# Weight pieces of 1 MB stored in four column blocks: each partition's row read as four runs of 2 KB in place of one of 8 KB

## The reference, cut to what matters

```python
scores = sigmoid(x @ router_w)                     # 32 experts, 8 of them chosen per row
gate = ragged_dot(xs, w_gate, group_sizes)         # xs: rows sorted by expert; w_gate [32, 1024, 512]
up   = ragged_dot(xs, w_up, group_sizes)
down = ragged_dot(silu(gate) * up, w_down, group_sizes)   # w_down [32, 512, 1024]
routed = (down[unsort].reshape(T, K, H) * tkw[..., None]).sum(axis=1)
shared = silu(x @ sw_gate) * (x @ sw_up) @ sw_down        # one shared expert, twice as wide
```

## Time and profile before

| | |
|---|---|
| median of 3 executions | 11513.4 us (11511.07 to 11513.97) |
| the profiled execution's own time | 11510.14 us |
| its span in the profile | 11508.5 us |
| busy: PE, DVE, POOL, ACT | 97%, 40%, 38%, 25% of the span |
| mean granted TensorE clock | 0.99 |
| moved by DMA | 1487 MB, 129 GB/s over the span |

### The profile page before, as it was taken

The page is one execution under the profiler, slowest core; times in us unless marked ns, Lnnn a source line. Parts: engine busy times, 40 slices in busy tenths (PEclk is TensorE's granted clock), DMA queues, the critical chain, the costliest instruction groups (busy, mean ns, idle before and its releaser), DMA issues.

```text
span 11508.5 us, 205338 instructions
## 1 busy us (share of the span) xinstructions
PE 11219.1 (97%) x49954; PEld 9236.2 (80%) x49955; DVE 4614.2 (40%) x6242; ACT 2927.2 (25%) x3904; POOL 4352.1 (38%) x4232
## 2 busy tenths in 40 slices
PE   8999899998999999999999999999999999999998
PEld 7888677776888888888888878878887887888887
DVE  5777766664233223332323242233334324223222
ACT  1111344442222222222222232222223223222221
POOL 2666532223333333333333333333433333333332
PEclk9999999999999999999999999999999999999999
DMA  5555567664444444454544454444556545444443
GB/s 185 169 168 174 156 181 179 180 181 136 96 119 117 98 97 118 119 138 110 125 97 118 97 159 95 111 122 118 126 141 172 126 109 144 97 97 117 97 97 84
DMA packets 954681, 1487.13 MB, mean 129 GB/s; under 512 B 318494, under 2 KB 621790, under 8 KB 930756
## 3 DMA queue, kind: packets, MB, share of 16 engines
q0 software_dynamic: 212224, 620.97, 25.3%
q1 hardware_dynamic: 356964, 474.75, 13.2%
q10 hardware_dynamic: 385376, 390.15, 12.1%
HBM read 887.22 MB, written 598.24 MB: 129 GB/s over the span
## 4 chain that ended last, share of the span: by engine, by line
PE 67%; DVE 3%; DMA 2%; issue 2%; ACT 1%; DVEq 1%; ACTq 0%; POOL 0%; SPq 0%; POOLq 0%
PE pd L2083 23%; PE pg L66 7%; PE pg L67 7%; PE pu L68 7%; PE pg L68 7%; PE pu L67 7%; PE pu L66 7%; DVE w_lo L1984 2%; DMA activated<-av 2%; DVEq L1658 1%; ACT w_hi L1891 1%; DMA aq<-activated 0%; ACT x_hi L1895 0%; ACTq L1658 0%; DVE aT L2006 0%
## 5 line engine op out<-in xcount | busy, mean ns | idle before, releaser
L1853 POOL DMA_INDIRECT out_rows<-y,idx_s x528 | 860.2, 1629 | 4444.7 <-issue 4434.7
L1845 POOL DMA_INDIRECT xq<-xn_rows,idx_q x2124 | 2141.0, 1008 | 934.2 <-issue 484.5
L1895 ACT ACTIVATE x_hi<-xT 128x1024 fp32r<-128x1024 f32 x530 | 562.9, 1062 | 4549.4 <-DMA activated<-av 4390.3
L66 PE MATMUL pg<-w_hi,x_hi 128*128 128x512 f32 x4224 | 1647.5, 390 | 42.2 <-DVE x_lo L1999 31.7
L66 PE MATMUL pu<-w_hi,x_hi 128*128 128x512 f32 x4224 | 1646.1, 390 | 1.2 <-DVEq L2053 0.4
L68 PE MATMUL pg<-w_hi,x_lo 128*128 128x512 f32 x4224 | 1646.5, 390 | 0.0
L67 PE MATMUL pg<-w_lo,x_hi 128*128 128x512 f32 x4224 | 1646.4, 390 | 0.0
L68 PE MATMUL pu<-w_hi,x_lo 128*128 128x512 f32 x4224 | 1645.0, 389 | 0.0
L67 PE MATMUL pu<-w_lo,x_hi 128*128 128x512 f32 x4224 | 1644.8, 389 | 0.0
L2034 DVE SCALAR_TENSOR_TENSOR av<-pu,scale,sg 128x512 f32<-128x512 f32 x528 | 396.4, 751 | 3067.5 <-PE pu L68 2955.7
L1999 DVE TENSOR_TENSOR x_lo<-xT,x_hi 128x1024 fp32r<-128x1024 f32 x530 | 649.6, 1226 | 1535.1 <-ACT x_hi L1895 1534.9
(11 more groups left out here) (292 smaller groups left out, 14665.0 us busy)
## 6 DMA issues: line engine op xcount, KB each, us to landing
stage<-in_w_all SPq DMA_DIRECT2D x174, 1024.0 KB, 9.0
activated<-av ACTq DMA_DIRECT2D x528, 256.0 KB, 2.3
aq<-activated ACTq DMA_DIRECT2D x528, 256.0 KB, 2.6
rep<-steps ACTq DMA_DIRECT2D x192, 512.0 KB
sums<-out_rows SPq DMA_DIRECT2D x68, 512.0 KB, 7.9
out_rows<-sums SPq DMA_DIRECT2D x68, 512.0 KB, 4.0
xq<-xn_rows,idx_q POOLq DMA_INDIRECT x2124
xt<-in_x SPq DMA_DIRECT2D x64, 512.0 KB, 6.2
```

What stands on the lines that cost most here:

```text
L66: m(dst, hi, whi[:, cols], start=begin, stop=False)
L1845: g.indirect_dma_start(out=xq[q][:, n], out_offset=None, in_=xn_q, in_offset=bass.IndirectOffsetOnAxis(ap=idx_q[q][:, n:n + 1], axis=0))\
L1853: g.indirect_dma_start(out=out, out_offset=bass.IndirectOffsetOnAxis(ap=idx_s[q][:, 0:1], axis=0), in_=y[q][:], in_offset=None, compute_op ...
L1895: a.activation(x_hi[q][:].rearrange("p b (g j) -> p b g j", g=4), xT[:].rearrange("p (g b j) -> p b g j", g=4, b=KH), ACT.Copy).then_inc(x ...
```

## The change

`w_all` is stored on the host as [pieces, 4, 128, 512] in place of [pieces, 128, 2048]: the first 512 columns of all 128 partitions, then the next 512, and so on. A piece is still 1 MB in one stretch, but the row of one partition now lies in it as four runs of 2 KB, 256 KB apart. The buffers on the chip, `raw` and `stage`, keep their layout; the four kinds of load name the four runs. Nothing else is changed: the same 186 transfers, by the same queues, at the same places, with the same waits.

```diff
+def pieces(tile):
+    return tile[:].rearrange("p (a c) -> p a c", a=4)
@@ route_stage, SP
-                sp.dma_start(raw[q][:], w_all[(E + 1) * NCH + q]).then_inc(w_loaded[q], 16)
+                sp.dma_start(pieces(raw[q]), w_all[(E + 1) * NCH + q].rearrange("a p c -> p a c")).then_inc(w_loaded[q], 16)
@@ route_stage, ACT
-                a.dma_start(raw[q][:], w_all[E * NCH + q]).then_inc(w_loaded[q], 16)
+                a.dma_start(pieces(raw[q]), w_all[E * NCH + q].rearrange("a p c -> p a c")).then_inc(w_loaded[q], 16)
@@ expert_stage, SP, load
-                    sp.dma_start(stage[q][:], w_all[bass.ds(e * NCH + q, 1)]
-                                 .rearrange("a p c -> (a p) c")).then_inc(staged[q], 16)
+                    sp.dma_start(pieces(stage[q]), w_all[bass.ds(e * NCH + q, 1)]
+                                 .rearrange("z a p c -> p (z a) c")).then_inc(staged[q], 16)
@@ expert_stage, SP, before the first tile
-                sp.dma_start(stage[q][:], w_all[bass.ds(e * NCH + q, 1)].rearrange("a p c -> (a p) c"))\
+                sp.dma_start(pieces(stage[q]), w_all[bass.ds(e * NCH + q, 1)].rearrange("z a p c -> p (z a) c"))\
                     .then_inc(staged[q], 16)
@@ layouts
-        "w_all": np.concatenate([*gu, dn], axis=1).reshape(n * NCH, P, WC),
+        "w_all": np.concatenate([*gu, dn], axis=1).reshape(n * NCH, P, 4, WC // 4).transpose(0, 2, 1, 3),
```

## The result

The changed kernel took 11533.9 us (median of 19 runs, 11529.2 to 11539.7), the kernel before 11513.1 us in the runs beside it (19 runs): 20.8 us more, a ratio of 1.0019 with an interval of [1.0013, 1.0025]. The prediction was 11446 us, with a range from 11418 to 11515. It was wrong in sign, and the result lies outside the range.

What follows compares the result with a forecast made beforehand. PE, busy 97% of the span, was taken as the bound, so only its stops could be won: 23 + 9 + 14 + 15 + 4 + 5 - 3 = 67 us off 11513.4 gave 11446 us, range 11418 to 11515.

Steps and rivals of the forecast that it cites:

- Rows: In the weight loads: 186 loads of 128 rows become 186 of 512, and the four runs are not joined again.
- rival C: Weight loads: the queue joins the runs, packets stay 8 KB and nothing happens; 11513 us, chance 0.04.
- Time of a row: On a DMA engine: 84 ns per 2 KB row, so a piece takes 2.70 us in place of 2.53.
- Turns: Between DMA queues: a row waits for one row of the other queue, 84 ns with 2 KB rows.
- roomy switches: Expert switches with room around them: about 20 PE gaps of 0.5 to 1.2 us; 15 us gained.
- Standing behind: Read of `aq` behind rows already taken on: depth counted in rows, so 0.7 us in place of 2.5.
- tight switch: Where one-tile experts follow each other: 4.5 of a 5.36 us gap gained; 23 us in all, 9 for slow clock.
- Rival A: At expert switches: depth is one of bytes or time, so gaps hardly move; about 11502 us, chance 0.21.
- The tile behind: Tile after a switch between one-tile experts: gaps of 2.81 and 1.30 us and slow matmuls; 14 of 25 us gained.
- The start: Kernel start: SP's rows wait less behind ACT's loads, so DVE begins 5 us earlier, passed on whole.
- Longer loads: Weight loads: six pieces take 1.0 us more DMA time, hidden since ACT doesn't wait; 3 us charged over the span.
- Rival B: At every switch: 2 KB rows cost 129 ns, the store finds more ahead; +40 us, 11553, chance 0.13.

Runs made afterwards that it cites:

- padded rows: Changed kernel with two unused 2 KB rows behind each block, runs 260 KB apart in place of 256: 11512.3 us, 1.0003 of the kernel before.
- the burst is split: Three pieces asked for ahead, the fourth a tile later: 11478.2 us with the 8 KB rows of before, 11508.3 with the changed layout, 11491.0 with runs 260 KB apart.
- near layout: Changed kernel with a partition's four 2 KB runs side by side, 2.25 KB apart: 11516.5 us, 1.0006 of the kernel before.
- repetition: Changed kernel run once more, unaltered, in the last batch: 11535.5 us, 1.0024 of the kernel before.

## Why the prediction was wrong, step by step

- **Rows.** Right: +95232 packets; rival C is out.
- **Time of a row.** Right where nothing else runs: 392 GB/s at 3293 to 3295 us against 388 foreseen, and a median row of 84 ns.
```profile
3293.00:3295.00 2.00, 2.00 (x11) 1.65 (x10) 1.02 (x2) 0.63 (x1) 1.06 (x3) 1.00 1.02 392
```
- **Turns.** Right, and better than it was used. It was applied to ACT's transfers against SP's loads. For POOL the text said that its gathers and adds "get a larger share beside loads: nothing but safety". **This is the first step that failed.** A larger share for POOL is a smaller one for the pieces, and the store stands behind the pieces. With padded rows, where the turns are left and the distance is not, the roomy switches lose 7 us in place of winning 15 (14.2 to 21), and where the burst is split the turns cost 13 us.
- **Standing behind.** **The second step that failed.** Depth was taken in rows (0.7 us). From a store's issue at a tight switch to its first row some 10 rows of 8 KB passed on an engine in the mean before the change, 20 of 4 KB, and 36 to 39 of 2 KB after it or in the near layout; the first row came after 3.7 to 3.9 us before, 3.6 to 3.8 in four of five with 4 KB, and 4.0 to 4.2 after. It is one of bytes or time, and which of these is open. Rival A had this right. The 46 us that the tight switches and the tiles behind them were to give hang on this step: with padded rows, without any loss by distance, these tiles stood at 90.8 us against 91.5 before.
- **The tight switch.** Foreseen: store 0.9 us and read 3.6 us less. Over five of these switches the store took 40.6 us in place of 36.5 (0.8 more each) and the read 29.6 in place of 37.3 (1.5 less each). Rival A had said 0 and 1.8. At the first:
```profile
7492.47 8.05 DMA activated<-av
7500.54 5.81 DMA aq<-activated
```
```profile
7507.98 2.05 PE L2089 MATMUL pd<-w_hi,a_hi 128*128 128x512 f32 x4 [4.97 <-ACT a_hi L1917]
7530.30 1.74 PE L2089 MATMUL pd<-w_hi,a_hi 128*128 128x512 f32 x4 [2.80 <-ACT a_hi L1917]
7532.77 2.07 PE L2089 MATMUL pd<-w_lo,a_hi 128*128 128x512 f32 x4 [0.73 <-DVEq L2032]
```
  The gap went from 5.36 to 4.97 us, not to under 1.5. The 9 us for the clock behind it did not come: the matmuls there still take 2.05 us for four. The tile behind has 2.80 and 0.73 us in place of 2.81 and 1.30. All such tiles together got 7.4 us worse, against 46 foreseen as gain.
- **The roomy switches.** Foreseen as 15 us gained, measured as 23 us lost (9.1 and 13.8). Some 7 of these are the turns with POOL, the other 16 the distance, the third failed step (below).
- **The start.** 5 us foreseen, 2 measured (1.0 in the repetition). `wcat` landed in 11.1 us and the queue of SP was held for 6.5 in place of 15.0 us, as the turns said; but DVE's product waits for the last small row, `bias_b`, which still ended behind ACT's pieces:
```profile
0.95 9.49 ACTq L583 DMA_DIRECT2D raw<-in_w_all  x6
2.50 6.52 SPq L393 DMA_DIRECT2D lnw_sb<-in_lnw  x1
21.14 0.96 DVE L709 TENSOR_TENSOR wcat<-sxq,lnw_sb 128x768 f32<-128x768 f32 x1 [19.83 <-DMA bias_b<-in_rbias]
```
- **Longer loads.** 3 us charged for the pieces. Right that ACT does not wait for them (7 waits as before, 53.3 us against 50.3, of which 1.0 more at the stage's beginning); wrong that this is all that a slow piece costs.
- **Rival B** had the place (every switch), the sign and the victim (the store), for the wrong reason: it wanted 129 ns a row, and rows take 84. **The third step that failed** is the distance of 256 KB, a term that the sum has at nothing: beside B stood a loss at large power-of-two distances, put at 0.1 us a piece and given no chance of its own. It carries most of the loss: 17 to 23 us with four pieces, 17 with three. B's 129 ns were a mean over a stretch: the median row of `aq` took 84 ns in the trace before, too.

What the sum should have been: 17 to 23 us for the distance (changed less padded kernel), a price that no row of before shows, and some 4 us for all else (padded kernel less before, an interval of -8 to +14). That these 4 are what is left of the turns with POOL after the cheaper reads and the earlier start is argued, not shown. Even without the distance, then, the 67 us were never there. One reading in the working was off too: eight matmuls at full clock take 1.8 us, not 2.1; it would have made the forecast gain larger by 1 to 2 us.

Left open: what exactly collides at 256 KB, why only in some stretches of a burst, and why two rows of 4 KB at 512 KB do not; for 2 KB rows only 2.25, 256 and 260 KB were tried.

## What to carry to other kernels

If queues take turns by row, a queue's share is the time of one of its rows over the sum of one row of each queue. Before cutting one queue's rows to make it polite towards a small transfer, list every other queue that runs beside it: the one with the longest rows takes what is given up, and a transfer that stands behind the cut queue pays. When a short transfer collides with a burst, move or shorten the burst (here 30 us for one piece asked for later) rather than its rows, and if blocks of 2 KB rows must lie apart, try a few KB on top of a distance that is a power of two (here 4 KB on 256).

## What the runs showed of the hardware that was not expected

- Turns are one row each, 104 to 104 in one stretch, over rows of 2 and 4 KB, and 76 to 77 over 8 and 4 KB; POOL's 4 KB rows take 309 ns in the mean with the adds and 212 without them (half as many rows), by which a row of an add takes an estimated 406 ns, if the gathers' rows take the same in both; an 8 KB row of a piece takes 309 (median) or 345 (mean).
- What stands ahead of a newly issued transfer did not shrink when the rows ahead became four times smaller: its first row came after some 3.8 us with 10 rows of 8 KB ahead of it and some 4.1 us with 38 of 2 KB.
- 2 KB rows 256 KB apart: 274 and 248 GB/s with partly idle engines in two stretches of a burst; 260 KB apart: 354 and 375; 4 KB rows 512 KB apart: 430 and 360.
- An issuing queue is held for longer with more rows: ACT's six loads at the start 9.5 us together in place of 3.2 (10.4 in the repetition), and 22.5 us with 1 KB rows.
